# Softmax denominators of a graph attention layer as columns, inverted there and spread by TensorE; the second projection in two passes; the residual's bias added on VectorE

## The reference

```python
def _gat_layer(x, src, dst, W, a_src, a_dst, bias, concat):
    h = (x @ W).reshape(N, H, C)
    al_s = einsum('nhc,hc->nh', h, a_src); al_d = einsum('nhc,hc->nh', h, a_dst)
    e = leaky_relu(al_s[src] + al_d[dst], 0.2)
    m = segment_max(e, dst)
    ex = exp(e - m[dst])
    denom = segment_sum(ex, dst)
    out = segment_sum(h[src] * (ex / (denom[dst] + 1e-16)), dst)
    return out + bias
h  = elu(_gat_layer(layernorm(x), W1 768x(4*512), ..., concat=True))    # 4 heads of 512
x  = x + _gat_layer(h, W2 2048x768, 1 head of 768)
x  = x + moe(layernorm(x))      # 8 experts, top 2, capacity, plus a shared expert
```

## Time and profile before

| what | value |
|---|---|
| time, median of 3 (lowest to highest) | 1327.04 us (1319.58 to 1328.58) |
| profiled execution, its own time | 1322.85 us |
| its span | 1321.1 us |
| granted TensorE clock, mean | 0.967 |
| PE busy | 1207.5 us (91%), 7111 matmuls |
| DVE busy | 873.4 us (66%) |
| ACT busy | 609.4 us (46%) |
| POOL busy | 161.9 us (12%) |
| layer 1's groups (first att to last) | 212.5 to 641.5 us |
| second projection | 641.5 to about 802 us |
| second attention | to 907 us |

### The profile page before, as it was taken

The page is one execution under the profiler, slowest core; times in us unless marked ns, Lnnn a source line. Parts: engine busy times, 40 slices in busy tenths (PEclk is TensorE's granted clock), DMA queues, the critical chain, the costliest instruction groups (busy, mean ns, idle before and its releaser), DMA issues.

```text
span 1321.1 us, 18384 instructions
## 1 busy us (share of the span) xinstructions
PE 1207.5 (91%) x7111; PEld 802.9 (61%) x7111; DVE 873.4 (66%) x1766; ACT 609.4 (46%) x1108; POOL 161.9 (12%) x144
## 2 busy tenths in 40 slices
PE   4887778888999799999999999999998799999996
PEld 3665443444555455545788888888556566666664
DVE  7889879988997899898543652444786323333330
ACT  5679356476546554876403650102311144444441
POOL 1000000000000000000000004000103734333322
PEclk9998999988999899999999999998999899999999
DMA  8344530462145323412753206213201587677532
GB/s 185 125 143 145 147 97 20 122 164 81 44 129 158 89 57 102 124 36 78 267 158 103 78 15 178 70 41 102 72 1 47 160 225 180 171 177 181 162 63 32
DMA packets 70210, 149.66 MB, mean 113 GB/s; under 512 B 10629, under 2 KB 34693, under 8 KB 69498
## 3 DMA queue, kind: packets, MB, share of 16 engines
q1 hardware_dynamic: 63467, 131.23, 33.2%
q0 software_dynamic: 6656, 17.26, 6.8%
HBM read 115.88 MB, written 34.59 MB: 114 GB/s over the span
## 4 chain that ended last, share of the span: by engine, by line
PE 58%; DVE 21%; issue 6%; ACT 6%; DMA 4%; SPq 2%; POOL 2%; POOLq 0%; DVEq 0%; ACTq 0%
PE PS L1775 47%; PE PS L1918 6%; DVE sb L1421 3%; DVE sb L1400 3%; DVE sb L1436 2%; DVE sb L1429 2%; SPq L541 2%; DVE sb L1288 1%; DVE sb L1470 1%; DVE sb L1371 1%; DVE sb L1481 1%; DMA sb<-aa_d 1%; POOL sb L850 1%; DMA sb<-in_L_ffn_w_dram 1%; DVE sb L1317 1%
## 5 line engine op out<-in xcount | busy, mean ns | idle before, releaser
L1775 PE MATMUL PS<-sb,sb 128*125 128x384 f16 (+8 forms) x4404 | 780.5, 337 | 45.3 <-DVE sb L1293 27.0
L1775 PEld LDWEIGHTS PS<-sb,sb 128*125 128x125 f16 (+3 forms) x4404 | 541.0, 128 | 269.0 <-issue 55.6
L1918 PE MATMUL PS<-sb,sb 125*128 125x375 f16 (+1 forms) x1440 | 263.1, 343 | 0.0
L1918 PEld LDWEIGHTS PS<-sb,sb 125*128 125x128 f16 x1440 | 140.5, 98 | 119.7 <-issue 9.5
L1619 DVE SCALAR_TENSOR_TENSOR sb<-sb,sb 128x2304 f16<-128x2304 f32 x27 | 68.8, 2557 | 84.5 <-ACT sb L1143 84.5
L1016 ACT ACTIVATE sb<-sb 125x375 f32<-125x375 f32 (+1 forms) x150 | 81.4, 543 | 83.6 <-DVE sb L1421 83.2
L830 POOL TENSOR_TENSOR sb<-sb,sb 125x768 f32<-125x768 f32 x10 | 18.0, 1838 | 803.2 <-DMA sb<-in_x_dram 803.2
L1421 DVE SCALAR_TENSOR_TENSOR sb<-sb,sb,sb 125x375 f32<-125x375 f32 (+1 forms) x150 | 95.6, 638 | 5.6 <-ACT sb L1010 5.4
L1010 ACT ACTIVATE sb<-sb,sb 125x375 f32<-125x375 f32 (+1 forms) x150 | 93.7, 628 | 0.7 <-DMA sb<-aa_d 0.7
L1429 DVE SCALAR_TENSOR_TENSOR sb<-sb,sb 125x375 f32<-125x375 f32 (+1 forms) x150 | 87.7, 585 | 1.2 <-ACT sb L1016 1.1
L1436 DVE TENSOR_TENSOR sb<-sb,sb 125x375 f16<-125x375 f32 (+1 forms) x150 | 87.9, 586 | 0.1
(11 more groups left out here) (188 smaller groups left out, 1062.0 us busy)
## 6 DMA issues: line engine op xcount, KB each, us to landing
sb<-in_L_ffn_w_dram SPq DMA_DIRECT2D x24, 1152.0 KB, 5.7
sb<-in_L_gnn_W_dram SPq DMA_DIRECT2D x32, 384.0 KB, 4.6
sb<-xt_d SPq DMA_DIRECT2D x30, 375.0 KB, 4.9
sb<-mask_d SPq DMA_DIRECT2D x20, 546.9 KB
sb<-h_d SPq DMA_DIRECT2D x10, 1000.0 KB, 5.4
h_d<-sb SPq DMA_DIRECT2D x16, 375.0 KB, 4.8
sb<-aa_d SPq DMA_DIRECT2D x5, 1093.8 KB
h_d<-sb SPq DMA_DIRECT2D x8, 500.0 KB, 5.0
```

The source lines that it names most:

```text
L1775: ins = M(out_, lhs(a), rhs(b), start=first and a + b == 0, stop=last and a == 1)
L1918: ins = M(PS[:, t, 0:n], hb[:, i, pa, 128 * c:128 * c + 128], P[:, i, pb, lo:lo + n], start=i == 0 and pa + pb == 0, stop=i == NT - 1 and ...
```

## The change

Four edits. (1) The denominators of a block: each 125x125 piece of P is now the stationary operand and one column of ones the moving one, so 2 x 10 matmuls of one column for each destination tile, 80 or 60 a block instead of 20 (`denominators`), into a few columns of bank 6. DVE inverts 125 x 4 or 125 x 3 values (`den_read`). TensorE spreads them: at the start of group c = 1 (BROADCAST_AT), 4 or 3 fp32 matmuls with the inverse column repeated as stationary operand and the identity as the moving one, into bank 4; ACT copies that to RDEN (`inverses_copy`). Groups c keep a bank each. For heads 0 to 2 `den_read` of block 1 moves ahead into g = 4, before the last two maxima. (2) `al2` and `al2_columns` go: W2S gets four more columns (V2 hi, V2 lo), written by a small DVE copy in `w2_lo`, and the second projection gives the attention sums as its first two output columns. (3) The second projection runs over all ten tiles for columns 0..321, then again for the other 448 (order 9, 2..8, 0, 1), with eight places for H1 tiles (five in P's space), six PSUM banks, and 12 tile loads instead of 10; `chain_row(H)`, maxima, `chain_shift(H)` and the P steps move into the second pass. (4) The bias is added on DVE (`x_bias`), not on GpSimd.

```diff
+        HALF_A = list(range(NT))
+        HALF_B = [9, 2, 3, 4, 5, 6, 7, 8, 0, 1]
+        HT_SLOT = [0, 1, 3, 4, 5, 6, 7, 2, 1, 0, 2, 1]
...
+            return (6, 7, 0, 1, 2, 3)[u % 6]
...
-        W2_STEPS = [0, 0, 0, 0, 0, 0, 1, 1, 1, 2, 2, 2, 2, 2, 2]
+        W2_STEPS = [0, 0, 0, 0, 0, 1, 1, 2, 2, 2, 2, 2, 2, 1, 0]
-        P2_STEPS = [0, 0, 0, 0, 6, 6, 6, 6, 6, 2]
+        BROADCAST_AT = (1, 0)
+        P2_STEPS = [0] * (NT + 4) + [5, 5, 5, 5, 6, 0, 6]
...
+                if h == H and b == 0:
+                    act.wait_ge(s_pj2, NT + 2 + min(4, (4 * N * i + 4 * N - 1) // 8000))
...
+            def inverses_copy(h, b):
+                n = DB[b][1]
+                act.wait_ge(s_rb, NB * h + b + 1)
+                A(RDEN[:, 0:n], PS[:, 4, 0:n], ACT.Copy).then_inc(s_rc, 1)
...
             def den_read(h, b):
-                a = NG * h + (CH + 1) * b
-                n = DB[b][1]
-                dve.wait_ge(s_att, a + 1)
-                V.reciprocal(RDEN[:, 0:n], PS[:, a % 4, 0:n]).then_inc(s_rd, 1)
+                k = NB * h + b
+                dve.wait_ge(s_att, NG * h + (CH + 1) * b + 1)
+                if k >= 2:
+                    dve.wait_ge(s_rb, k - 1)
+                V.reciprocal(RC[:, k % 2, 0:len(TB[b])], PS[0:T, 6, 0:len(TB[b])]).then_inc(s_rd, 1)
...
                 if c == 0:
-                    dve.wait_ge(s_rd, NB * h + b + 1)
+                    dve.wait_ge(s_rc, NB * h + b + 1)
...
+            def x_bias(j):
+                if j == 0:
+                    dve.wait_ge(s_bias, 48)
+                dve.wait_ge(s_xr[j], 32)
+                V.tensor_tensor(X2[:, j, :], X2[:, j, :], B2R[:, :], ALU.add).then_inc(s_xb, 1)
...
+            def denominators(h, b):
+                k = NB * h + b
+                if k == 0:
+                    pe.wait_ge(s_mm, NT)
+                else:
+                    pe.wait_ge(s_rd, k)
+                if b == 0 and h + 1 < H:
+                    pe.wait_ge(s_hl, NT * (h + 2) - 1)
+                for i in range(NT):
+                    pe.wait_ge(s_p6, step(h, b, i) + 1)
+                    for j in TB[b]:
+                        for part in range(2):
+                            col = j - TB[b].start
+                            ins = M(PS[0:T, 6, col:col + 1], P[:, i, part, T * j:T * j + T], ones[:, 0:1],
+                                    start=i == 0 and col == 0 and part == 0,
+                                    stop=i == NT - 1 and j == TB[b][-1] and part == 1)
+                ins.then_inc(s_att, 1)
+
+            def inverses_broadcast(h, b):
+                k = NB * h + b
+                pe.wait_ge(s_rd, k + 1)
+                if k:
+                    pe.wait_ge(s_y1, CH * k)
+                for col in range(len(TB[b])):
+                    ins = M(PS[:, 4, T * col:T * col + T], RC[:, k % 2, col:col + 1].to_broadcast([T, 128]),
+                            idf[0:T, 0:T], start=True, stop=True)
+                ins.then_inc(s_rb, 1)
...
-                if c == CH - 1 and NB * h + b:
-                    al2(NB * h + b - 1)
...
+            for u in range(2 * NT):
+                q = u // NT
+                ht, arrived, value = ht_use(u)
                 pe.wait_ge(arrived, value)
...
+                    if u == NT and ch == 4:
+                        chain_row(H)
+                    if u == NT + 3 and ch == 8:
+                        chain_shift(H)
```

More of the change, by code:

```diff
@@ L223, in build @@
     FS = small([85, 2], F32)
+    RC = small([T, 2, 4], F32)
     flag = small([128, 1], I32)
@@ L350, in build @@
         s_att = sem("attention_group_done")
-        s_rd = sem("denominator_made")
+        s_rd = sem("denominators_inverted")
+        s_rb = sem("inverses_broadcast")
+        s_rc = sem("inverses_copied")
         s_y1 = sem("y_divided")
@@ L820, in _ @@
             link(nc.gpsimd.memset(big[:, :], -NEG))
-            link(nc.gpsimd.memset(SEL[:, :, :], 0.0))
-            for part in range(2):
-                link(nc.gpsimd.affine_select(out=SEL[:, :, :], in_=SEL[:, :, :], compare_op=ALU.not_equal, fill=1.0,
-                                             base=-2 * part, pattern=[[-4, NB], [-1, 2]], channel_multiplier=1))
-            pool.wait_ge(s_bias, 48)
-            for j in range(NT):
-                pool.wait_ge(s_xr[j], 32)
-                nc.gpsimd.tensor_tensor(X2[:, j, :], X2[:, j, :], B2R[:, :], ALU.add).then_inc(s_xb, 1)
             pool.wait_ge(s_at2, NT)
@@ L1115, in _ @@
             A(WRS[:, :, 0, :], WRG[:, :, :], ACT.Copy, scale=SW).then_inc(s_wh, 1)
-            for j in range(NT):
-                p_steps(H, P2_STEPS[j])
-                h2_hi(j)
+            for u in range(2 * NT):
+                p_steps(H, P2_STEPS[u])
+                h2_hi(u)
+            p_steps(H, P2_STEPS[2 * NT])
             assert p_made[H] == NT * NB + 2
@@ L1611, in _ @@
                                 ALU.mult).then_inc(s_xn2, 1)
+                if j + 1 < NT:
+                    x_bias(j + 1)
                 if j:
@@ L1844, in proj @@
                         pe.wait_ge(s_hl, NT * h + i - 1)
+                    if h >= 2 and i == 0:
+                        pe.wait_ge(s_rd, NB * (h - 1))
                     for k in range(KD):
@@ L1909, in att @@
                         chain_shift(amid)
-                    if c < 0:
-                        pe.wait_ge(s_p6, step(h, b, i) + 1)
-                        for part in range(2):
-                            ins = M(PS[:, t, 0:n], ones[:, :], P[:, i, part, lo:lo + n],
-                                    start=i == 0 and part == 0, stop=i == NT - 1 and part == 1)
-                    else:
-                        hb = HB[h % 2]
-                        for pa, pb in ((0, 0), (0, 1), (1, 0)):
-                            ins = M(PS[:, t, 0:n], hb[:, i, pa, 128 * c:128 * c + 128],
-                                    P[:, i, pb, lo:lo + n], start=i == 0 and pa + pb == 0,
-                                    stop=i == NT - 1 and pa == 1)
-                        if c == CH - 1 and i < NT - 1:
-                            ins.then_inc(s_pf, 1)
@@ L1923, in att @@
-                ins.then_inc(s_att, 1)
-            def al2(k):
-                h, b = divmod(k, NB)
-                n, nj = DB[b][1], len(TB[b])
-                pe.wait_ge(s_y6, CH * (k + 1))
-                if k in (0, NB * (H - 1)):
-                    pe.wait_ge(s_vs, 1 if k == 0 else 2)
-                for c in range(CH):
-                    for part in range(2):
-                        ins = M(PS[0:12, 4, 0:n], V2S[:, CH * h + c, 8 - 4 * b:20 - 4 * b],
-                                H1O[k % 2][:, part, 0:nj, c, :], start=k + c + part == 0,
-                                stop=k == NB * H - 1 and c == CH - 1 and part == 1)
-                ins.then_inc(s_a2, 1)
@@ L1938, in al2_columns @@
-            def al2_columns():
-                pe.wait_ge(s_const, 16)
-                pe.wait_ge(s_a2r, 1)
-                for b in range(NB):
-                    for j in TB[b]:
-                        lo = T * (j - TB[b].start)
-                        ins = M(PS[0:T, 5, 2 * j:2 * j + 2], A2W[:, lo:lo + T], SEL[:, b, :], start=True, stop=True)
-                ins.then_inc(s_a2c, 1)
+                    if (c, i) == BROADCAST_AT:
+                        inverses_broadcast(h, b)
+                    for pa, pb in ((0, 0), (0, 1), (1, 0)):
+                        ins = M(PS[:, c, 0:n], hb[:, i, pa, 128 * c:128 * c + 128],
+                                P[:, i, pb, lo:lo + n], start=i == 0 and pa + pb == 0,
+                                stop=i == NT - 1 and pa == 1)
@@ L1947, in _ @@
+                    if c == CH - 1 and i < NT - 1:
+                        ins.then_inc(s_pf, 1)
+                ins.then_inc(s_att, 1)
             for h in range(H):
@@ L1999, in _ @@
                 b = 4 + 2 * (j % 2)
-                for i in range(NT):
+                order = HALF_B if j == 0 else HALF_A
+                for i in order:
                     if j == 0:
-                        pe.wait_ge(s_h2l, 3 * (i + 1))
+                        pe.wait_ge(s_h2l, h2_made(NT + HALF_B.index(i)))
                     for b_ in range(NB):
```

242 lines of the change are left out of this document (120 added, 122 removed).

## The result

The changed kernel takes **1330.68 us** (median of 18 runs, 1321.09 to 1337.47) where the kernel before takes 1326.38 on the same chips: ratio 1.0039, 95% interval 1.0023 to 1.0054. That is within 1% of no change, and by its interval slightly slower. The forecast was 1312 (1299 to 1326), so the time lies outside the range, on the other side of no change.

A forecast was written before the change was run, and what follows sets the result against it. DVE was taken to bound the second two thirds of each layer 1 head, TensorE the rest. Layer 1 -8.2 and second projection -4.1 gave -12.3 us: 1312, between 1310.5 and 1314.7; 8-in-10 range 1299 to 1326.

The forecast's parts named there:

- the clock: Behind denominator groups TensorE falls to 1.2 GHz, costing 1.3 to 1.7 us each where it bounds, nothing where it waits.
- Pairs at 55.6 ns: Denominators: weight load plus one-column matmul priced by the router's row, so groups take 4.4 and 3.3 us.
- slower: Rival, denominators in heads 1 to 3: pairs cost 113 ns, +25 us net, 1337; decides from 91 ns; chance 0.10.
- Reciprocals: DVE's twelve denominator reciprocals, 33.1 us in all before, take 0.2 us each; ACT's new copy 0.5 to 0.6.
- The stop of 5.7 us in head 3: Head 3, block 0: TensorE stands 5.7 us for DVE's reciprocal before c = 1, where before it went on.
- In heads 0 to 2 the reciprocal comes in time: Spreading the inverses in heads 0 to 2: TensorE does not have to wait for DVE's reciprocal.
- Head 2 the same: -3.1: Layer 1, head 2: as head 1, +1.3 us in block 0, then -4.4 for two reciprocals, net -3.1.
- -1 each: Heads' ends, twice: TensorE's stop shrinks from 7.6 to about 3 us, leaving less time at 1.2 GHz.
- Second projection, -4.1: Second projection: +0.4 us for more columns, -5.0 for attention sums and their clock fall, 0.5 wait for W2.
- The bias, nothing: Second attention: bias on DVE, 10 x 0.78 us, costs nothing since TensorE bounds and DVE is half busy.
- More comes back: Rival, layer 1: the clock does not fall behind groups or the head 3 stop; -9 us, 1303; chance 0.15.
- Held up: Rival: gain goes into TensorE's waits for inverses and late W2 chunks or H1 tiles; -2, 1322; chance 0.18.

The follow-up runs named there:

- e1: Changed kernel with each denominator matmul's moving operand 128 columns of ones instead of one, only the first read: 1318.45 us, ratio 0.995 to the kernel before.
- e4: Changed kernel with W2's chunks split earlier and W2 chunk 11 loaded ahead of the first H1 tile: 1327.95 us, ratio 1.0026 to the kernel before.
- e5: e1 with W2's chunks split earlier, all 16 ahead of head 3's last group, first H1 tile loaded behind chunk 12: 1316.72 us, ratio 0.9937.
- e11: Changed kernel with the bias added on GpSimd again instead of DVE: 1328.08 us, ratio 1.0023 to the kernel before.
- e7: Changed kernel with edit (1) undone (20 row denominator matmuls, large reciprocals), edits (2) to (4) kept, plus e5's earlier W2 chunks: 1326.12 us, ratio 1.0.
- e6: e5 with the inverses of head 3's block 0 spread at the start of c = 2 instead of c = 1: 1308.5 us, ratio 0.9867.
- e2: Changed kernel with one-column matmuls dealt out among c = 0's dense ones, inverses spread in the middle of c = 1: 1376.33 us, ratio 1.0393.

## Why the prediction was wrong, step by step

Times at which the same work starts (us in the trace). The forecast column is before plus the prediction's own sums (8.0 us for layer 1, as its items give; its total has 8.2).

| place | before | forecast | after | e1 |
|---|---|---|---|---|
| end of head 0, projection goes on | 314.1 | 310.4 | 311.5 | 309.1 |
| end of head 1, projection goes on | 442.0 | 434.2 | 441.9 | 434.2 |
| head 3, c = 0 | 561.5 | 549.5 | 564.3 | 551.1 |
| first pass of the second projection | 641.3 | 633.5 | 646.1 | 635.5 |
| transposes behind attention tile 2 | 822.9 | 810.8 | 829.6 | 818.6 |

e1 is within 2 us of the forecast at all four places up to the first pass, the changed kernel leaves the forecast in head 1 and ends layer 1 12.6 us behind it.

- **The step that failed: the clock.** "I expect a fall behind each group of 80 and behind two in three of the groups of 60, each costing 1.3 to 1.7 us". The place was right; the size was not. The sum has one fall of 1.6 us in head 1. Measured against e1, the fall at the group of 80 cost 4.8 us (1.9 in the group, 2.8 behind it), and the two that the sum put at nothing cost 1.6 and 3.2: 9.6 us. The row I took the size from the earlier trace rows stands behind 20 small matmuls, with 1.2 GHz for 3.4 us behind them; here 80 follow each other, with about 10 us. I had asked whether a clock fall comes, and took its length from one case. The router's row beside it was the closer one, 81 small matmuls and 1.2 GHz behind them: from 907 to 940 us that trace has a mean clock of 0.74, which is 17 us at the low one.
- With 9.6 us in head 1 TensorE used up the 7.6 us that it had stood at the head's end, and the waits turned: 1.43 us there instead of my "about 3". From there on TensorE was the bound, and the 4.4 us a head that the sum took off VectorE's chain were worth nothing. "Nothing where it waits anyway" held only while there was wait left.
- **Pairs at 55.6 ns: nearly right.** Groups of 60 took 3.59 us at full clock for a forecast of 3.3, and groups of 80 4.80 with 128 columns for 4.4: 60 ns a pair. The rival "slower" gave a price of 91 ns and more a pair as its condition. Its total, 1337, is the nearest of the three rivals to the 1330.7 measured, but its condition did not hold on the whole: in the groups of 80 that ran into 1.2 GHz early a pair took 84 ns in head 1 (6.74 us) and 91 in head 0 (7.29 us), in the other whole groups 60 to 70, and most of head 1's loss lies in the dense groups behind, which that rival did not price. The weight load of 104 ns by the Trainium skill (TensorE: Matmul & The Clock Gate, LDWEIGHTS) did not set the pace here either, since load and matmul together took 60 ns.
- **Reciprocals: right**, 0.17 to 0.18 us each; the copy 0.47 and 0.58, the spreading 1.05 for block 0 and 0.83 for the others.
- **The stop of 5.7 us in head 3**: it did not come in the changed kernel (0.34 us), because TensorE was late by then. In e1 it stood there with 5.66 us, so the step was right for the kernel that I had reckoned with. "In heads 0 to 2 the reciprocal comes in time" was not quite: e1 also waits 1.06 and 0.33 us for inverses in head 0, 2.26 in head 1, and 3.06 in block 2 of head 3.
- **"Head 2 the same: -3.1"** and **"-1 each" at the heads' ends**, -4.1 from the end of head 1 to head 3's c = 0: -2.6 in e1, +2.9 after.
- **Second projection, -4.1: the work was right, the wait not.** I took 0 to 1 us for W2's last chunk; it was 3.90, over the 3 us that the prediction itself named as a sign of being wrong, as was the group of 80 with over 6 us:

```profile
646.09 6.35 PE L1813 MATMUL PS<-sb,sb 128*125 128x322 f16 x45
656.33 4.02 PE L1813 MATMUL PS<-sb,sb 128*125 128x322 f16 x14 [3.90 <-DVE sb L1529]
```

I had let the chunk be ready 6 to 7 us into the pass, and it came at 10.2. The chain shows what I left out, the load of a chunk that is issued behind 1 MB of H1, with ScalarE and then VectorE waiting for it (start us, us, what):

```profile
631.79 8.05 DMA sb<-in_L_gnn_W_dram
639.86 0.85 ACT sb L1100
640.82 0.95 DVE sb L1529
```

Behind these rows the chain runs on for 15 us over ScalarE and VectorE, through the last groups' reads with the other chunks between them. e4 moved a load and the splits together, so it does not tell how much of the lateness each is.

- In e5, where that wait is gone, the stretch takes 176.9 us against 181.6: -4.7 for a forecast of -4.1. H1 tiles and P steps: hidden, no wait over 0.3 us.
- **The bias, nothing**: not contradicted; no effect can be told (e11).
- **The rivals.** "More comes back", no falls, was to give 1303. e1 has no more low clock in layer 1 than the kernel before (25 us against 30) and yet reaches the forecast's milestones, not the rival's, 9 us earlier. Its condition is met only in part, since the stop in head 3 has a fall behind it in e1 too; but where the falls are gone VectorE sets the pace, and TensorE waits 7.4 us for h_lo at the heads' ends and 12.4 for the inverses. Most of the other 6 us between e1 and 1312 are the second projection with its wait (183.1 us for a forecast of 177.5). "Held up", 1322, did not occur in layer 1: TensorE's waits for the inverses are 1.1 us there in the changed kernel. Its late W2 chunk did, with 3.9 us.

What stays open: how the 28 us of work that e1 won back split between the falls inside the groups, behind them and behind the stops; and what part 1 and parts 2 to 4 are worth each once VectorE is relieved, since no run has the column denominators without the other parts. Parts 2 to 4 with row denominators give nothing (e7). The columns, 128 wide, on top of them give 0.6% (e5 against e7), with the passes' wait for W2 in e7 counted in, and with the late spreading 1.3% (e6). As they were made, one column wide, they take 0.3% (e4 against e7, intervals that overlap, and one chunk of W2 later in e4).

## What to carry to other kernels

Price a run of small matmuls twice: by its own length, and by the clock it leaves to the dense work behind it. In head 1 the clock took 9.6 us where the change was to gain 3.1, and such a loss is paid in full once TensorE has no wait left to hide it. If load and matmul of a pair cost the same with one column as with 128, widen the moving operand with columns nobody reads. And put as much of TensorE's own work as the banks allow between a small result's inputs and the wait for it: in e2, with half a group between them, eight waits took 30.2 us, and e6 won back 4 to 8 us by moving one wait of 5.7.
